# Slice stage of a graph network on one core: small attention's maximum and sums on ScalarE, z at the end of VectorE's step, output in the tokens' bank, slice tokens turned behind the logits

## The chip, the cores and the metric

The kernel runs on one core of one Trainium2 chip. The metric is the device time of the whole program in microseconds: 2829.99 us, the median of three runs from 2829.58 to 2830.06 us. An instruction stream runs on each engine: TensorE (PE, with its weight loads as PEld), VectorE (DVE), ScalarE (ACT), GpSimd (POOL) and SyncE (SP). They wait for each other by semaphores that the program sets by hand.

## What is computed

The input is x, 128 graphs of 128 nodes with 128 features in fp32, and an adjacency matrix for each graph. Four blocks are added to x in turn, each behind a layer norm: graph attention with an MLP, attention over slices, a graph convolution, and a mixture of experts. The change touches the second block alone, which is, for each graph with 8 heads of 64 columns:

```python
fx_mid = (x @ W_fx + b_fx).reshape(B, N, H, D).transpose(0, 2, 1, 3)
x_mid = (x @ W_x + b_x).reshape(B, N, H, D).transpose(0, 2, 1, 3)
slice_weights = jax.nn.softmax((x_mid @ W_slice + b_slice) / temp, axis=-1)
slice_token = jnp.einsum('bhnc,bhng->bhgc', fx_mid, slice_weights)
slice_token = slice_token / (slice_weights.sum(axis=2)[..., None] + 1e-05)
q, k, v = slice_token @ W_q, slice_token @ W_k, slice_token @ W_v
attn = jax.nn.softmax(jnp.einsum('bhgc,bhkc->bhgk', q, k) * SCALE, axis=-1)
out_slice = jnp.einsum('bhgk,bhkc->bhgc', attn, v)
out_x = jnp.einsum('bhgc,bhng->bhnc', out_slice, slice_weights)
return out_x.transpose(0, 2, 1, 3).reshape(B, N, INNER) @ W_out + b_out
```

The "small attention" is the softmax over 64 x 64 slices of each head (`attn`).

## The kernel before

All 128 graphs stay in on-chip memory as `X`. Five functions run one after the other: `attention_phase`, `mlp_phase`, `slice_phase`, `graph_phase`, `expert_phase`. At the end of `mlp_phase` some weights for the slice stage are made once, among them `wscore`, the product of W_q and W_k that turns slice tokens into keys (L588).

`slice_phase` is a software pipeline over graphs, written out by hand: in step t every engine works on several graphs, each at another point of its way, and does its pieces always in the order in which the code lists them. `run_steps` (L33) writes eight steps ahead, a loop of two steps, and seven behind. `live(known, n, ...)` says that a piece of step t works on graph t - n. There is no scheduler; a wait stands in front of the piece that needs it, and every piece behind it on that engine waits too. Some waits keep TensorE from writing a PSUM bank that another engine still reads.

TensorE's step t, by name and line:

1. logits of graph t-2 (L88 to L90, three matmuls of 512 columns) into `ps_l`
2. keys of graph t-4 (L882): the transposed tokens times `wscore`, into `ps_t`
3. transposes of `share`, the small attention's probabilities, of graph t-5 (L890) into `ps_h`
4. fx of graph t-2 (again L88 to L90) into `ps_f`
5. behind nine waits (L897 to L915), transposes of the slice weights `sw` of graph t-4 (L916)
6. scores of graph t-4 (L922), mixed of t-6 (L929), mt of t-5 (L936), u of t-3 (L947: the slice tokens before they are divided by their norm; `ps_u` lies in the bank of the logits)
7. transpose of z, the normalized graph t-1 (L956), into a bank of `ps_x`
8. output of graph t-6 (L965 and L968) into `ps_x`; it waits for ScalarE's copy of `mixed`
9. transposes of the tokens `tok` of graph t-3 (L976); it waits for VectorE's `tok`

ScalarE's step copies PSUM to SBUF and takes exponentials: key (L988), shareT (L993), expo (L998), mixed (L1005), att (L1010, the small attention's exponential over 256 columns at once), fx (L1016), zTh (L1021), mt (L1024), swT (L1029), tokT (L1034). VectorE's step: top and diff of the logits (L1051, L1055), z (L1062), statistics, top2 and diff2 of the scores (L1081, L1085), sum and reciprocal of expo (L1092, L1094), tok (L1098 to L1105), zTl (L1110), sum and reciprocal of att (L1116, L1118), the addition of the output to X (L1122), statistics. GpSimd's step: sw (L833), share (L840), rstd (L847, L850), and the statistics for the next stage (L856 to L860).

The maximum of the scores is taken off in VectorE (`diff2`), and ScalarE applies the factor 64 ** -0.5 in the exponential:

```python
nc.vector.reduce_max(top2[:, :, :], ps_s, AX.X).then_inc(s["top2_done"], 1)
...
nc.scalar.activation(att[:, :, :], diff2[:, :, :], ACT.Exp,
                     scale=float(C) ** -0.5).then_inc(s["att_done"], 1)
```

Of the kernel before, what the change touches and what calls it, by code (L numbers as in the profile page):

```python
# [15 lines left out]
D = 128  # L16
# [6 lines left out]
C = 64  # L23
# [487 lines left out]
def mlp_phase(nc, sem, sh, n_graphs):  # L511

    groups = n_graphs // GB
    with ExitStack() as ctx:
# [68 lines left out]
        def _(act):  # L583
# [4 lines left out]
            nc.scalar.activation(sh.wscore[:, :], ps_m, ACT.Copy).then_inc(wscore_copied, 1)  # L588
# [166 lines left out]
def slice_phase(nc, sem, sh, n_graphs):  # L755

    with ExitStack() as ctx:
# [6 lines left out]
        def ps(name, shape):  # L764
# [25 lines left out]
        diff2 = sb("s_diff2", [128, HP, C])  # L790
# [9 lines left out]
        ps_out, ps_z = ps_x[:, 0, 2 * C:2 * C + D], ps_x[:, 1, 2 * C:2 * C + D]  # L800
# [9 lines left out]
                 "scores_done top2_done diff2_done att_done sum2_done rsum2_done share_done share_turned shareT_done "  # L810
# [9 lines left out]
        def _(pool):  # L820
# [7 lines left out]
            def step(t, r, p, known):  # L828
                if live(known, 2, n_graphs):
# [13 lines left out]
                if live(known, 0, n_graphs):  # L843
                    pool.wait_ge(s["meanvar_done"], t + 1)
                    if since(known, 2):
                        pool.wait_ge(s["z_done"], t - 1)
                    nc.gpsimd.tensor_tensor(rstd[p][:, 1:2], meanvar[p][:, 1:2], sh.eps[:, 0:1],  # L847
                                            ALU.add).then_inc(s["eps_added"], 1)
                    pool.wait_ge(s["eps_added"], t + 1)
                    nc.gpsimd.tensor_tensor(rstd[p][:, 0:1], rstd[p][:, 1:2], sh.half_power[:, 0:1],  # L850
                                            ALU.pow).then_inc(s["rstd_done"], 1)
# [13 lines left out]
        def _(pe):  # L865
# [3 lines left out]
            def step(t, r, p, known):  # L869
                q = 1 - p  # L870
                if live(known, 2, n_graphs):

# [7 lines left out]
                if live(known, 4, n_graphs):  # L880
                    pe.wait_ge(s["tokT_done"], t - 3)
                    nc.tensor.matmul(ps_t[:, 0:2, :], sh.wscore[:, :], tokT[p][:, :, :], start=True,  # L882
                                     stop=True).then_inc(s["keys_done"], 1)
                if live(known, 5, n_graphs):
                    pe.wait_ge(s["share_done"], t - 4)
                    if since(known, 6):
                        pe.wait_ge(s["shareT_done"], t - 5)
                    pe.wait_ge(s["zT_done"], t - 1 if known is None else min(known - 1, n_graphs))
# [8 lines left out]
                if live(known, 4, n_graphs):  # L897
                    pe.wait_ge(s["key_copied"], t - 3)
                    if since(known, 5):
                        pe.wait_ge(s["diff2_done"], t - 4)  # L900
                    if since(known, 7):
                        pe.wait_ge(s["x_done"], t - 6)
                    if live(known, 2, n_graphs):
                        pe.wait_ge(s["zT_done"], t - 1)
                if live(known, 5, n_graphs):
                    pe.wait_ge(s["shareT_done"], t - 4)
                    if since(known, 7):
                        pe.wait_ge(s["mixed_copied"], t - 6)
                if live(known, 6, n_graphs):
                    pe.wait_ge(s["mt_copied"], t - 5)  # L910
                if live(known, 4, n_graphs):
# [5 lines left out]
                    last.then_inc(s["sw_turned"], 1)  # L917
                if live(known, 4, n_graphs):
# [31 lines left out]
                if live(known, 1, n_graphs):  # L950
                    pe.wait_ge(s["z_done"], t)
                    if since(known, 2):
                        pe.wait_ge(s["zT_done"], t - 1)
                    if live(known, 4, n_graphs):
                        pe.wait_ge(s["diff2_done"], t - 3)
                    nc.tensor.transpose(ps_z, z[:, :], sh.ident[:, :]).then_inc(s["z_turned"], 1)  # L956
                if live(known, 6, n_graphs):
                    pe.wait_ge(s["mixed_copied"], t - 5)
                    pe.wait_ge(s["swT_done"], t - 5)
                    if live(known, 4, n_graphs):  # L960
                        pe.wait_ge(s["diff2_done"], t - 3)
# [9 lines left out]
                if live(known, 3, n_graphs):  # L971
                    pe.wait_ge(s["tok_done"], t - 2)
                    if live(known, 4, n_graphs):
                        pe.wait_ge(s["key_copied"], t - 3)
                    for j in range(2):
                        last = nc.tensor.transpose(ps_t[:, j, :], tok[q][:, 2 * j:2 * j + 2, :], sh.ident[:, :])  # L976
                    last.then_inc(s["tok_turned"], 1)
# [3 lines left out]
        def _(act):  # L981
            def step(t, r, p, known):
                q = 1 - p
                if live(known, 4, n_graphs):
                    act.wait_ge(s["keys_done"], t - 3)
                    if since(known, 5):
                        act.wait_ge(s["scores_done"], t - 4)
                    nc.scalar.activation(key[:, :, :], ps_t[:, 0:2, :], ACT.Copy).then_inc(s["key_copied"], 1)  # L988
                if live(known, 5, n_graphs):
# [3 lines left out]
                    nc.scalar.activation(shareT[:, :, :], ps_h[:, :, :], ACT.Copy).then_inc(s["shareT_done"], 1)  # L993
                if live(known, 2, n_graphs):
# [3 lines left out]
                    nc.scalar.activation(expo[p][:, :, :], diff[p][:, :, :], ACT.Exp).then_inc(s["expo_done"], 1)  # L998
                if live(known, 6, n_graphs):
# [6 lines left out]
                if live(known, 4, n_graphs):  # L1006
                    act.wait_ge(s["diff2_done"], t - 3)
                    if since(known, 5):
                        act.wait_ge(s["share_done"], t - 4)
                    nc.scalar.activation(att[:, :, :], diff2[:, :, :], ACT.Exp,  # L1010
                                         scale=float(C) ** -0.5).then_inc(s["att_done"], 1)
# [5 lines left out]
                if live(known, 1, n_graphs):  # L1017
                    act.wait_ge(s["z_turned"], t)
                    if since(known, 3):
                        act.wait_ge(s["fx_done"], t - 2)  # L1020
                    nc.scalar.activation(zTh[q][:, :], ps_z, ACT.Copy).then_inc(s["zTh_done"], 1)  # L1021
# [8 lines left out]
                if live(known, 3, n_graphs):  # L1030
                    act.wait_ge(s["tok_turned"], t - 2)
                    if since(known, 5):
                        act.wait_ge(s["scores_done"], t - 4)
                    nc.scalar.activation(tokT[q][:, :, :], ps_t[:, 0:2, :], ACT.Copy).then_inc(s["tokT_done"], 1)  # L1034
# [3 lines left out]
        def _(dve):  # L1038
# [8 lines left out]
            def step(t, r, p, known):  # L1047
# [10 lines left out]
                if live(known, 1, n_graphs):  # L1058
                    dve.wait_ge(s["rstd_done"], t)
# [1260 lines left out]
```

## Time and profile before

| | |
|---|---|
| median of three runs | 2829.99 us (2829.58 to 2830.06) |
| span of the profiled execution | 2829.7 us |
| mean granted TensorE clock | 0.985 |
| TensorE busy | 2695.7 us, 95% of the span |
| VectorE busy | 1966.7 us, 70% |
| ScalarE busy | 1461.8 us, 52% |
| GpSimd busy | 1503.5 us, 53% |
| slice stage, VectorE's first maximum of scores to its last | 800.5 to 1630.1 us |

The times of the profiled execution are those of one run under the profiler; the runs without it agree with its span to 0.4 us. Rows of the timeline give the start, the duration, the engine, the line, what is written and what is read, and how many like instructions are merged in the row. A duration is longer than the time that an instruction holds its engine, because the next one may start while it ends; so what an instruction costs in a chain of like ones is read from start to start.

### The profile page before, as it was taken

Reading aid. Unit: us, or ns where it says so; the run is one execution under the profiler, and the core shown is the slowest. Engines: PE = TensorE matmul, PEld = TensorE weight load, DVE = VectorE, ACT = ScalarE, POOL = GpSimd, SP = SyncE. Lnnn points to the kernel's source line nnn. Section 1 sums busy time; section 2 is a strip of 40 time slices with the busy share of each in tenths; the row PEclk is TensorE's granted clock in tenths of the full one; section 3 lists DMA queues with packets and bytes.
Section 4 is the critical chain, followed back from the end, with each engine's and each line's share of the span. In section 5 each row is a group of like instructions: output and inputs, shape, how many; then the busy total and the mean of one; then the engine's idle time right before and its main releaser. Section 6 shows DMA issues by size and latency. Waiting matters only on the chain. (4 is left out here: it accounts for less than half of the span.)

```text
span 2829.7 us, 87893 instructions
## 1 busy us (share of the span) xinstructions
PE 2695.7 (95%) x28783; PEld 2136.2 (75%) x28784; DVE 1966.7 (70%) x6881; ACT 1461.8 (52%) x2930; POOL 1503.5 (53%) x2542
## 2 busy tenths in 40 slices
PE   8999999899989999999999989999998999999999
PEld 4666666599957777777777767777778999999988
DVE  5666666577778888888888858788874454545453
ACT  3444444455546666666666535455554444444444
POOL 5555555333234444444444427777761666666674
PEclk8999999999989999999999999999999999999999
DMA  1111111000000000000000011111232222222264
GB/s 52 30 37 30 36 31 46 3 0 0 0 1 0 0 0 0 0 0 0 0 0 0 1 35 58 57 56 56 85 115 61 75 76 81 75 80 77 71 195 147
DMA packets 158090, 118.01 MB, mean 42 GB/s; under 512 B 20150, under 2 KB 145593, under 8 KB 158010
## 3 DMA queue, kind: packets, MB, share of 16 engines
q1 hardware_dynamic: 140602, 81.02, 10.4%
q0 software_dynamic: 17408, 35.95, 3.8%
q8 instruction: 46, 0.75, 0.1%
q14 instruction: 34, 0.28, 0.0%
HBM read 68.36 MB, written 48.56 MB: 41 GB/s over the span
## 5 line engine op out<-in xcount | busy, mean ns | idle before, releaser
L2025 POOL DMA_INDIRECT token_y<-e_y,e_rows x288 | 294.7, 1023 | 78.8 <-issue 73.1
L2068 ACT ACTIVATE e_hidden<-e_ps,e_b1g 128x512 f32<-128x512 f32 x288 | 194.6, 688 | 258.4 <-PE e_ps L90 257.8
L833 POOL TENSOR_TENSOR s_sw<-s_expo,s_rsum 128x512 f32<-128x512 f32 x128 | 133.5, 1043 | 355.4 <-DVE s_rsum L1094 355.4
L1301 POOL DMA_INDIRECT sorted_z<-r_z,r_rows x256 | 264.8, 1034 | 66.6 <-issue 61.8
L2120 PE MATMUL e_ps<-expert_w,e_hidden 128*128 x2304 | 280.3, 275 | 0.0
L460 DVE TENSOR_REDUCE a_V<-a_ps_s 128x8 f32<-128x1024 f32 x128 | 156.9, 1226 | 176.8 <-PE a_ps_s L399 176.8
L2120 PEld LDWEIGHTS e_ps<-expert_w,e_hidden 128*128 128x128 f32 x2304 | 273.9, 192 | 6.3
L324 ACT ACTIVATE a_probT<-a_ps_st 128x1024 f32<-128x1024 f32 x128 | 131.2, 1025 | 203.3 <-PE a_ps_st L407 203.3
L399 PEld LDWEIGHTS a_ps_s<-a_nT 16*128 16x128 f32 x2048 | 136.2, 188 | 91.5 <-issue 55.6
L2197 DVE TENSOR_TENSOR e_biased<-e_ps,expert_b 128x512 f32<-128x512 f32 x72 | 49.8, 691 | 213.8 <-PE e_ps L2120 213.8
L399 PE MATMUL a_ps_s<-a_nT 16*128 16x128 f32 x2048 | 185.6, 299 | 11.1
L407 PE MATMUL a_ps_st<-a_topT,a_nT 17*128 17x128 f32 x2048 | 183.6, 297 | 0.1
L1005 ACT ACTIVATE s_mixed<-s_ps_v 128x512 f32<-128x512 f32 x128 | 76.5, 598 | 148.6 <-PE s_ps_v L936 145.8
L968 PE MATMUL s_ps_x<-s_mixed,s_swT 128*128 128x128 f32 x1024 | 143.6, 284 | 0.0
L407 PEld LDWEIGHTS a_ps_st<-a_topT,a_nT 17*128 17x128 f32 x2048 | 134.7, 186 | 1.1 <-issue 0.6
L608 ACT ACTIVATE m_hidden<-m_ps,m_b 128x512 f32<-128x512 f32 x128 | 86.8, 689 | 87.3 <-PE m_ps L90 87.2
L88 PE MATMUL e_ps<-e_zTh,e_w1h 128*128 128x512 f32 x288 | 126.5, 439 | 1.6 <-DVE e_zTl L2189 1.4
L968 PEld LDWEIGHTS s_ps_x<-s_mixed,s_swT 128*128 128x128 f32 x1024 | 127.1, 195 | 0.0
L660 PE MATMUL m_ps<-m_w,m_hidden 128*128 128x128 f32 x1024 | 124.4, 275 | 0.0
L660 PEld LDWEIGHTS m_ps<-m_w,m_hidden 128*128 128x128 f32 x1024 | 121.7, 192 | 2.8
L1361 PE MATMUL g_ps_h<-ident_bf 128*128 128x512 bf16 x476 | 120.6, 385 | 3.1 <-PEq L104 3.1
L263 POOL TENSOR_TENSOR X<-X,a_attn 128x128 f32 (+1 forms) x128 | 60.1, 470 | 112.7 <-DVE a_attn L455 110.4
(400 smaller groups left out, 8033.8 us busy)
## 6 DMA issues: line engine op xcount, KB each, us to landing
e_z<-sorted_z SPq DMA_DIRECT2D x72, 260.0 KB
c_y<-token_y SPq DMA_DIRECT2D x22, 512.0 KB, 4.1
X<-in_x_dram SPq DMA_DIRECT2D x32, 256.0 KB, 2.8
a_adj<-in_adj_dram SPq DMA_DIRECT2D x32, 256.0 KB, 2.8
g_adj<-in_adj_dram SPq DMA_DIRECT2D x32, 256.0 KB
out_dram<-X SPq DMA_DIRECT2D x32, 256.0 KB, 2.6
c_y_s<-token_y SPq DMA_DIRECT2D x10, 512.0 KB, 5.0
token_y<-e_y,e_rows POOLq DMA_INDIRECT x288
```

Of the source, the lines that this page charges most:

```text
L88: nc.tensor.matmul(out, weights[0], moving[0], start=start, stop=False)
L324: nc.scalar.activation(probT[b % 2][:, :, :, :], ps_st[:, :, :, :], ACT.Exp, scale=float(HD) ** -0.5).then_inc(s["prob_done"], 1)
L399: last = nc.tensor.matmul(ps_s[:, j, 2 * half + c, :], side, side, start=False, stop=(half == 1 and c == 1))
L407: last = nc.tensor.matmul(ps_st[:, j, 2 * (1 - half) + c, :], nT[own][rows, i, c, :], topT[(b + 2) % 4][rows, c, :], start=False, stop=(ha ...
L460: nc.vector.reduce_max(V[p][:, b, :, TOP].rearrange("p (c i j) -> p j i c", c=2, j=2), ps_s[:, :, :, :].rearrange("p j (i c) n -> p j i c ...
L660: last = nc.tensor.matmul(ps_2[1 - p][:, b, :], hidden[1 - p][:, f, b * T:(b + 1) * T], w2[:, f, :], start=(f == 0), stop=(f == FC - 1))
L833: nc.gpsimd.tensor_tensor(sw[p][:, :, :], expo[p][:, :, :], rsum[p][:, 1, :].unsqueeze(2).to_broadcast([T, HEADS, C]), ALU.mult).then_inc( ...
L968: last = nc.tensor.matmul(ps_out, swT[p][:, 2 * j + i, :], mixed[:, i, j, :], start=False, stop=(j == 1 and i == 1))
L1301: nc.gpsimd.indirect_dma_start(sh.sorted_z, bass.IndirectOffsetOnAxis(ap=rows[own][:, e * GB + piece:e * GB + piece + 1], axis=0), zr[own] ...
L2025: nc.gpsimd.indirect_dma_start(sh.token_y, bass.IndirectOffsetOnAxis(ap=rows[p][:, b:b + 1], axis=0), y[p][:, b, :], None).then_inc(y_scat ...
L2068: nc.scalar.activation(hidden[p][:, c, :], ps_1[c % 2][:, :], ACT.Gelu, bias=b1g[p][:, c:c + 1]).then_inc(s["hidden_done"], 1)
L2120: last = nc.tensor.matmul(ps_2[q][:, b, :], hidden[q][:, f, b * T:(b + 1) * T], w2[:, bass.ds(e, 1), f * D:(f + 1) * D].squeeze(1), start= ...
```

## The change

The pieces and their counts stay, but for the small attention. Its factor goes into `wscore`. VectorE takes the maximum with its sign turned, and ScalarE takes four exponentials of 64 columns straight from the scores in PSUM, each with its own maximum as a bias and its own sum written out; `diff2` and VectorE's sum are gone. TensorE turns the tokens one step later, behind the logits, and makes the keys behind fx; z is transposed in front of the scores into the tokens' bank `ps_t`, where the output now stands too. z is made at the end of VectorE's step for the step after, and GpSimd makes rstd first.

```diff
@@ mlp_phase
-            nc.scalar.activation(sh.wscore[:, :], ps_m, ACT.Copy).then_inc(wscore_copied, 1)
+            nc.scalar.activation(sh.wscore[:, :], ps_m, ACT.Copy, scale=float(C) ** -0.5).then_inc(wscore_copied, 1)
@@ slice_phase
-        ps_out, ps_z = ps_x[:, 0, 2 * C:2 * C + D], ps_x[:, 1, 2 * C:2 * C + D]
+        ps_z, ps_out = ps_t[:, 2, :], ps_t[:, 3, :]
@@ TensorE: tokens behind the logits
+                    pe.wait_ge(s["tok_done"], t - 3)
+                    pe.wait_ge(s["zT_done"], upto(-1))
...
+                        pe.wait_ge(s["key_copied"], t - 4)
...
+                        pe.wait_ge(s["x_done"], t - 6)
+                    for j in range(2):
+                        last = nc.tensor.transpose(ps_t[:, j, :], tok[p][:, 2 * j:2 * j + 2, :], sh.ident[:, :])
+                    last.then_inc(s["tok_turned"], 1)
@@ TensorE: keys behind fx, then the transposes of sw, then these waits and z
+                    pe.wait_ge(s["tokT_done"], t - 3)
+                    nc.tensor.matmul(ps_t[:, 0:2, :], sh.wscore[:, :], tokT[p][:, :, :], start=True,
+                                     stop=True).then_inc(s["keys_done"], 1)
...
+                if live(known, 4, n_graphs):
+                    pe.wait_ge(s["key_copied"], t - 3)
+                    if since(known, 5):
+                        pe.wait_ge(s["att_done"], t - 4)
...
+                    nc.tensor.transpose(ps_z, z[:, :], sh.ident[:, :]).then_inc(s["z_turned"], 1)
@@ ScalarE: behind zTh, in front of mixed
+                    act.wait_ge(s["top2_done"], t - 3)
...
+                    for i in range(2):
+                        for e in range(2):
+                            last = nc.scalar.activation(att[:, 2 * i + e, :], ps_s[:, i, e, :], ACT.Exp,
+                                                        bias=top2[:, i, e:e + 1],
+                                                        accum_out=rsum2[:, 0, 2 * i + e:2 * i + e + 1])
+                    last.then_inc(s["att_done"], 1)
@@ VectorE
-                    nc.vector.reduce_max(top2[:, :, :], ps_s, AX.X).then_inc(s["top2_done"], 1)
...
-                    nc.vector.tensor_tensor(diff2[:, :, :].rearrange("p (i e) k -> p i e k", e=2), ps_s,
-                                            top2[:, :, :].unsqueeze(3).to_broadcast([128, 2, 2, C]),
-                                            ALU.subtract).then_inc(s["diff2_done"], 1)
+                    nc.vector.reduce_max(top2[:, :, :], ps_s, AX.X, negate=True).then_inc(s["top2_done"], 1)
+                if live(known, 1, n_graphs):
+                    dve.wait_ge(s["zTh_done"], t)
+                    nc.vector.tensor_tensor(zTl[q][:, :], ps_z, zTh[q][:, :], ALU.subtract)\
+                      .then_inc(s["zT_done"], 1)
...
-                    nc.vector.reduce_sum(rsum2[:, 0, :], att[:, :, :], AX.X).then_inc(s["sum2_done"], 1)
...
+                if live(known, 0, n_graphs):
+                    dve.wait_ge(s["rstd_done"], t + 1)
```

On TensorE, one step inside the loop stood as follows before, from the keys to the next step's logits (its second half; `s_ps_x`, `s_ps_t` and so on are the PSUM tiles that are written):

```order
L88 MATMUL s_ps_l<-s_wlogit_high,s_zTh 128x512
L89 MATMUL s_ps_l<-s_wlogit_low,s_zTh 128x512
L90 MATMUL s_ps_l<-s_wlogit_high,s_zTl 128x512
L882 MATMUL s_ps_t<-s_tokT,wscore 128x256
L890 MATMUL s_ps_x<-ident,s_share 128x128 x2
...
L916 MATMUL s_ps_w<-ident,s_sw 128x128 x4
L922 MATMUL s_ps_x<-s_key,s_tokT 64x64 x8
...
L956 MATMUL s_ps_x<-ident,s_z 128x128
L965 MATMUL s_ps_x<-out_bias,ones_bf 128x128
L968 MATMUL s_ps_x<-s_mixed,s_swT 128x128 x4
L976 MATMUL s_ps_t<-ident,s_tok 128x128 x2
```

And the same step now:

```order
L88 MATMUL s_ps_l<-s_wlogit_high,s_zTh 128x512
L89 MATMUL s_ps_l<-s_wlogit_low,s_zTh 128x512
L90 MATMUL s_ps_l<-s_wlogit_high,s_zTl 128x512
L887 MATMUL s_ps_t<-ident,s_tok 128x128 x2
L895 MATMUL s_ps_x<-ident,s_share 128x128 x2
...
L904 MATMUL s_ps_t<-s_tokT,wscore 128x256
L911 MATMUL s_ps_w<-ident,s_sw 128x128 x4
L924 REGISTER_ALU
L927 MATMUL s_ps_t<-ident,s_z 128x128
L932 MATMUL s_ps_x<-s_key,s_tokT 64x64 x8
...
L969 MATMUL s_ps_t<-out_bias,ones_bf 128x128
L972 MATMUL s_ps_t<-s_mixed,s_swT 128x128 x4
```

The tokens' transposes left the end of the step for its front, the keys went behind fx, and z went from behind u to a place between the transposes of sw and the scores.

On ScalarE, the same step before, from the exponential of the logits on:

```order
L998 ACTIVATE s_expo<-s_diff 128x512
L1005 ACTIVATE s_mixed<-s_ps_v 128x512
L1010 ACTIVATE s_att<-s_diff 128x256
L1016 ACTIVATE s_fx<-s_ps_f 128x8x64
L1018 REGISTER_ALU
L1021 ACTIVATE s_zTh<-s_ps_x 128x128
L1024 ACTIVATE s_mt<-s_ps_v 128x256
L1029 ACTIVATE s_swT<-s_ps_w 128x512
L1034 ACTIVATE s_tokT<-s_ps_t 128x256
```

And now (in the program the subtracted maximum and the sums, `top2` and `rsum2`, are shown as `s_top` and `s_rsum`):

```order
L1000 ACTIVATE s_expo<-s_diff 128x512
L1002 REGISTER_ALU
L1005 ACTIVATE s_zTh<-s_ps_t 128x128
L1013 ACTIVATE s_att,s_rsum<-s_ps_x,s_top 128x64 x4
L1023 ACTIVATE s_mixed<-s_ps_v 128x512
L1028 ACTIVATE s_fx<-s_ps_f 128x8x64
L1031 ACTIVATE s_mt<-s_ps_v 128x256
L1036 ACTIVATE s_swT<-s_ps_w 128x512
```

zTh and att now stand in front of mixed, att is four instructions instead of one, and tokT went to the front of the step.

## Rows read from the trace of the kernel before

**Rows 1.** Windows view, the slice stage's full steps: busy us and counts by engine
```profile
core 0: us, PE busy (x) PEld busy (x) DVE busy (x) ACT busy (x) POOL busy (x), PEclk, DMA share, GB/s
832.00:1558.00 726.00, 699.70 (x9994) 533.75 (x9994) 633.27 (x2223) 443.69 (x1111) 356.59 (x778) 1.00 0.00 0
```

**Rows 2.** Waits view, 900 to 1500 us: us in total, times, longest us
```profile
PEld s_ps_w L916 <- issue: 47.1, 90, 0.6
...
PEld s_ps_l L88 <- issue: 20.6, 46, 0.4
PEld s_ps_t L976 <- DVE s_tok L1105: 16.5, 92, 0.2
```

**Rows 3.** Timeline, TensorE, 1000 to 1014 us: start, duration, line, out<-in
```profile
1000.25 0.40 PE L90 MATMUL s_ps_l<-s_wlogit_high,s_zTl 128*128 128x512 f32 x1
...
1007.30 0.59 PE L882 MATMUL s_ps_t<-s_tokT,wscore 128*128 128x256 f32 x2
1007.73 0.38 PE L890 MATMUL s_ps_x<-ident,s_share 128*128 128x128 f32 x2
1007.87 0.48 PE L88 MATMUL s_ps_f<-s_wfx_high,s_zTh 128*128 128x512 f32 x1
...
1008.42 0.40 PE L90 MATMUL s_ps_f<-s_wfx_high,s_zTl 128*128 128x512 f32 x1
1008.88 0.63 PE L916 MATMUL s_ps_w<-ident,s_sw 128*128 128x128 f32 x4
1009.43 0.46 PE L922 MATMUL s_ps_x<-s_key,s_tokT 64*64 64x64 f32 x16
...
1011.11 0.33 PE L956 MATMUL s_ps_x<-ident,s_z 128*128 128x128 f32 x1
1011.36 0.23 PE L965 MATMUL s_ps_x<-out_bias,ones_bf 128*128 128x128 bf16 x1
...
1012.55 0.44 PE L976 MATMUL s_ps_t<-ident,s_tok 128*128 128x128 f32 x2
1012.75 0.50 PE L88 MATMUL s_ps_l<-s_wlogit_high,s_zTh 128*128 128x512 f32 x1
...
1013.31 0.40 PE L90 MATMUL s_ps_l<-s_wlogit_high,s_zTl 128*128 128x512 f32 x1
1013.56 0.70 PE L882 MATMUL s_ps_t<-s_tokT,wscore 128*128 128x256 f32 x2
```

**Rows 4.** Timeline, ScalarE, the same stretch
```profile
1008.01 0.39 ACT L988 ACTIVATE s_key<-s_ps_t 128x256 f32<-128x256 f32 x1 [1.15 <-PE s_ps_t L882]
1008.29 0.38 ACT L993 ACTIVATE s_shareT<-s_ps_x 128x256 f32<-128x256 f32 x1
1009.04 0.63 ACT L998 ACTIVATE s_expo<-s_diff 128x512 f32<-128x512 f32 x1 [0.37 <-DVE s_diff L1055]
1010.71 0.60 ACT L1005 ACTIVATE s_mixed<-s_ps_v 128x512 f32<-128x512 f32 x1 [1.04 <-PE s_ps_v L936]
1011.20 0.41 ACT L1010 ACTIVATE s_att<-s_diff 128x256 f32<-128x256 f32 x1
...
1011.99 0.28 ACT L1021 ACTIVATE s_zTh<-s_ps_x 128x128 fp32r<-128x128 f32 x1
1012.14 0.40 ACT L1024 ACTIVATE s_mt<-s_ps_v 128x256 f32<-128x256 f32 x1
```

**Rows 5.** Timeline, VectorE, the same stretch
```profile
1008.31 0.69 DVE L1055 TENSOR_TENSOR s_diff<-s_ps_l,s_top 128x512 f32<-128x512 f32 x1
...
1009.96 0.42 DVE L1081 TENSOR_REDUCE s_top<-s_ps_x 128x4 f32<-128x256 f32 x1
1010.51 0.42 DVE L1085 TENSOR_TENSOR s_diff<-s_ps_x,s_top 128x256 f32<-128x256 f32 x1
```

**Rows 6.** Groups of instructions: busy us, mean ns of one, idle before
```profile
L608 ACT ACTIVATE m_hidden<-m_ps,m_b 128x512 f32<-128x512 f32 x128 | 86.8, 689 | 87.3 <-PE m_ps L90 87.2
```

**Rows 7.** Timeline, ScalarE in the graph convolution, 1762 us
```profile
1762.07 0.19 ACT L1581 ACTIVATE r_odds<-r_gap 128x4 f32<-128x4 f32 x1
1762.17 0.58 ACT L1589 ACTIVATE g_y<-g_ps_y 128x512 f32<-128x512 f32 x1
```

More of the change, by code:

```diff
@@ L828, in step @@
             def step(t, r, p, known):
+                if live(known, 0, n_graphs):
+                    pool.wait_ge(s["meanvar_done"], t + 1)
+                    if since(known, 2):
+                        pool.wait_ge(s["z_done"], t - 1)
+                    nc.gpsimd.tensor_tensor(rstd[p][:, 1:2], meanvar[p][:, 1:2], sh.eps[:, 0:1],
+                                            ALU.add).then_inc(s["eps_added"], 1)
+                    pool.wait_ge(s["eps_added"], t + 1)
+                    nc.gpsimd.tensor_tensor(rstd[p][:, 0:1], rstd[p][:, 1:2], sh.half_power[:, 0:1],
+                                            ALU.pow).then_inc(s["rstd_done"], 1)
                 if live(known, 2, n_graphs):
@@ L870, in step @@
                 q = 1 - p
+                upto = lambda n: t + n if known is None else min(known + n, n_graphs)
                 if live(known, 2, n_graphs):
@@ L970, in step @@
                     last.then_inc(s["out_done"], 1)
[L971 to L977, printed above, removed]
             run_steps(pe, step, n_graphs, LAG, PEEL)
@@ L984, in step @@
                 if live(known, 4, n_graphs):
[L985 to L988, printed above, removed]
+                    act.wait_ge(s["tok_turned"], t - 3)
+                    if since(known, 6):
+                        act.wait_ge(s["scores_done"], t - 5)
+                    nc.scalar.activation(tokT[p][:, :, :], ps_t[:, 0:2, :], ACT.Copy).then_inc(s["tokT_done"], 1)
                 if live(known, 5, n_graphs):
@@ L993, in step @@
                     nc.scalar.activation(shareT[:, :, :], ps_h[:, :, :], ACT.Copy).then_inc(s["shareT_done"], 1)
+                if live(known, 4, n_graphs):
+                    act.wait_ge(s["keys_done"], t - 3)
+                    if since(known, 5):
+                        act.wait_ge(s["scores_done"], t - 4)
+                    nc.scalar.activation(key[:, :, :], ps_t[:, 0:2, :], ACT.Copy).then_inc(s["key_copied"], 1)
                 if live(known, 2, n_graphs):
@@ L998, in step @@
                     nc.scalar.activation(expo[p][:, :, :], diff[p][:, :, :], ACT.Exp).then_inc(s["expo_done"], 1)
+                if live(known, 1, n_graphs):
+                    act.wait_ge(s["z_turned"], t)
+                    if since(known, 3):
+                        act.wait_ge(s["fx_done"], t - 2)
+                    nc.scalar.activation(zTh[q][:, :], ps_z, ACT.Copy).then_inc(s["zTh_done"], 1)
+                if live(known, 4, n_graphs):
+                    act.wait_ge(s["top2_done"], t - 3)
+                    if since(known, 5):
+                        act.wait_ge(s["share_done"], t - 4)
+                        act.wait_ge(s["rsum2_done"], t - 4)
+                    for i in range(2):
[4 more added lines that the diff above has]
+                    last.then_inc(s["att_done"], 1)
                 if live(known, 6, n_graphs):
@@ L1005, in step @@
                     nc.scalar.activation(mixed[:, :, :, :], ps_m, ACT.Copy).then_inc(s["mixed_copied"], 1)
[L1006 to L1011, printed above, removed]
                 if live(known, 2, n_graphs):
@@ L1057, in step @@
                                             ALU.subtract).then_inc(s["diff_done"], 1)
-                if live(known, 1, n_graphs):
-                    dve.wait_ge(s["rstd_done"], t)
-                    if since(known, 2):
-                        dve.wait_ge(s["z_turned"], t - 1)
-                    nc.vector.tensor_scalar(z[:, 1:D], X[:, bass.ds(t - 1, 1), 1:D].squeeze(1), meanvar[q][:, 0:1],
-                                            rstd[q][:, 0:1], ALU.subtract, ALU.mult).then_inc(s["z_done"], 1)
                 counted = live(known, 0, n_graphs) or live(known, 7, n_graphs)
@@ L1126, in step @@
                       .then_inc(s["after_stats_done"], 1)
+                if live(known, 0, n_graphs):
+                    dve.wait_ge(s["rstd_done"], t + 1)
+                    if since(known, 1):
+                        dve.wait_ge(s["z_turned"], t)
+                    nc.vector.tensor_scalar(z[:, 1:D], X[:, bass.ds(t, 1), 1:D].squeeze(1), meanvar[p][:, 0:1],
+                                            rstd[p][:, 0:1], ALU.subtract, ALU.mult).then_inc(s["z_done"], 1)
             run_steps(dve, step, n_graphs, LAG, PEEL)
```

68 lines of the change are left out of this document (16 added, 52 removed).

## Prediction

> **What bounds the kernel now.** I read the page's first part, then the slice stage alone in the windows view, then its waits, then one step of it engine by engine in the timeline. The page's engine rows name TensorE as the busiest engine of the whole program; the question is whether that holds where the change is made. In the slice stage it is busy 699.7 of 726 us at full clock, VectorE 633.3, ScalarE 443.7 [rows 1]: TensorE is the bound there, and what the change takes off VectorE is worth nothing unless TensorE waits for it. The same row of TensorE's timeline stands at 1000.25 and at 1013.31 [rows 3]: two steps take 13.06 us, one 6.53. TensorE's idle time is 726 - 699.7 = 26.3 us in 111 steps, 0.24 us a step, though short starts after each wait hide a little more of it in "busy". The waits view says where: the weight load of L916 (0.51 us a step, partly beside matmuls), the loop's end at L88 in every second step, and L976 for the tokens, 16.5/92 = 0.18 us [rows 2]. So a change that only takes TensorE's waits away could win at most about 0.24 x 126 = 30 us.
>
> The second thing to see is who feeds the last block of TensorE's step. ScalarE ends `mixed` at 1010.71 + 0.60 = 1011.31 [rows 4], and the output matmuls (L965) start at 1011.36 [rows 3]. They start 0.05 us behind that copy: already now it is just in time, with the transpose of z as the only work in front of it.
>
> **The change, part by part.**
>
> *Maximum and sums.* VectorE loses the subtraction (0.42 us) [rows 5] and a sum over as many elements, some 0.8 us a step together, on an engine that is not the bound: worth nothing by itself. ScalarE gets four exponentials of 64 columns in place of one of 256, each with a bias column and a sum written out. The trace shows none with both, so I build the price from start to start. A copy of 256 columns holds the engine 0.28 us (1008.01 to 1008.29), one of 128 0.15 (1011.99 to 1012.14) [rows 4], so one of 64 about 0.09. A bias column adds 0.09: 689 ns against the 0.60 of `mixed`, the same size [rows 4, 6]. The Exp took 0.41 against the 0.38 of a copy of that size [rows 4]: 0.025. A sum that is written out I price as one more tiny instruction on the engine: one of four columns holds it 0.10 us (1762.07 to 1762.17) [rows 7]. Together 0.305, four of them 1.22 us where one instruction of 0.41 stood [rows 4]. The ends are 0.09 each (bias and sum free) and 0.5 each (a 64-column instruction of 0.28 - 0.065 + 0.09 and one of 0.19 with no overlap at all). I take 0.305, since every row of ScalarE that stands back to back does overlap.
>
> The Trainium skill, "ScalarE: Activation LUTs", section What ACT_TABLE_LOAD costs, gives 186 ns plus 0.833 ns a column, 93 ns more for a pointer operand, and 93 ns of overlap back to back. The trace agrees on the pointer (0.09 us). As an estimate from that page each of the four is 239 ns before any price for its sum, and the cycle below would be 7.10 us, 2902 us in all. The skill's "VectorE: DVE Perf Modes", section Two Vector instructions with no wait between them, says that on VectorE an operation that writes out its accumulator is two instructions; no run here shows whether ScalarE does the same.
>
> *ScalarE's order.* The four now stand in front of `mixed`, not behind it. Before, `mixed` needed only TensorE's L936; now it stands behind top2, which needs the scores, VectorE's maximum and the four exponentials. Queued behind it on ScalarE are fx, mt and swT, which nobody needs before the next step; TensorE's output waits for `mixed` itself. This is the term that decides.
>
> *TensorE's order.* The tokens' transposes move behind logits, keys behind fx, and between keys and the wait for their copy lie only the four transposes of sw (0.55 us, 1008.88 to 1009.43) [rows 3], where two transposes and fx stood before (0.14 + 0.80 = 0.94 us, worked out below). The wait for `shareT` is then long satisfied, and so is the one for tok. The loop's end comes behind eight output matmuls that are already queued, so its 0.45 us (20.6/46) [rows 2] in every second step goes too. But what is late next is the key copy, and then `mixed`.
>
> *z early, output in the tokens' bank, GpSimd's rstd first, the scale in the score weight.* z is made at the end of the step before, and TensorE asks for it only behind the transposes of sw; rstd needs only the statistics of the same step; the x addition, over half as many elements as the maximum of 0.42 us [rows 5], fits into the 0.81 us of logits that stand before the tokens' transposes into the same bank. I cost these at nothing. Were the addition late, the price would be at most those 0.42 us a step.
>
> *The sum.* In the changed order one cycle runs through TensorE, ScalarE, VectorE and back, and nothing else in the step is as long:
> - output to next logits: 1011.36 to 1012.55 less the 0.18 of waiting for tok: 1.01 [rows 2, 3]
> - logits 1012.75 to 1013.56: 0.81; two pairs of transposes at 0.14 (1007.73 to 1007.87): 0.28; fx 0.55 + 0.25 (1007.87 to 1008.42, last matmul as 1013.31 to 1013.56): 0.80 [rows 3]
> - start of keys to start of the copy, 1007.30 to 1008.01: 0.71; copy 0.39 [rows 3, 4]
> - from the copy's end (1008.40) to TensorE's next matmul took 0.48 with one register step and eight more waits to pass (1008.88) [rows 3, 4]; now fewer are left behind it, half: 0.25 (ends 0.1 and 0.48)
> - z, as 1011.11 to 1011.36: 0.25; scores' start to VectorE's maximum, 1009.43 to 1009.96: 0.53; maximum 0.42; to ScalarE 0.04 (1008.31 + 0.69 to 1009.04) [rows 3 to 5]
> - four exponentials: 1.22; `mixed` 0.60; to TensorE 0.05 [rows 4]
>
> That is 6.14 + 1.22 = 7.36 us against 6.53: 0.83 us more in each step that has both scores and output. Scores belong to steps 4 to 131 and output to steps 6 to 133, so 126 steps: 0.83 x 126 = 104 us. The other stages stay. Seen from TensorE: from the scores' start it can reach the output after about 1.7 us (1009.43 to 1011.11), `mixed` comes after 0.53 + 0.42 + 0.04 + 1.22 + 0.60 + 0.05 = 2.86; about 1.1 us of idling there and some 0.3 before z, less the waits that go.
>
> The profiled execution's span is 2829.7 us and the runs' median 2829.99, so what lies around the span is about 0.3 us. 2830 + 104 = **2934 us**.
>
> **The rivals.**
> - *The sums are dear.* Each sum holds ScalarE for a tiny instruction's whole 0.19 us [rows 7]: 0.395 each, 6.14 + 1.58 = 7.72 us, +150: 2980. For it: in rows 7 the neighbour reads something else, and no row shows an instruction that takes up what the one just before it has summed. Against it: that neighbour did start after 0.10.
> - *The sums are free.* Written by the same instruction: 0.205 each, 6.96 us, +54: 2884. For it: no row shows a sum that costs.
> - *The chain is hidden: no change.* At 0.09 each the cycle is 6.50 us, 4 us less in all: 2826. It needs bias and sum to cost nothing, against the rows of both [rows 6, 7].
> - *Faster, the other side.* TensorE's waits go and nothing takes their place: 0.24 us a step, 30 us: 2800. The place is L969's wait for `mixed`; it decides at 4 exponentials below 6.53 - 6.14 = 0.39 us in all. For it: 0.51 us of L916's idle weight load, 0.45 of the loop's end and 0.18 of L976 are real and do go [rows 2], and parts of my cycle may run closer together than their rows. Against it: even four bare copies of 64 columns take 0.36 us.
>
> **How the numbers follow.** Forecast 0.56; dear sums 0.19; free sums 0.15; hidden 0.04; faster 0.06. About 0.2% is what a measurement of this kernel can tell from no change. Faster 0.06, within it 0.04, slower 0.90. The range holds the forecast, the free and the dear sums with a little on each side: 2878 to 2988. With the ends of the wait after the key copy (-0.15 to +0.23 us a step, -19 to +29 us) the forecast alone is 2915 to 2963.
>
> **What would show it.** In the changed trace: TensorE's load of out_bias (L969) waits for ScalarE's `mixed` about 1 us in every step; a start-to-start of some 0.3 us for each of the four att instructions; ACT's mixed no longer waits for TensorE; a wait of TensorE at z (L927) for the key copy; the loop's end at L88 and the token wait gone; VectorE about 100 us less busy, with long waits for the scores; the steps 7.2 to 7.5 us apart. Wrong would be a step below 6.6 us, an output that does not wait for `mixed`, or a loss that stands in another stage.

## The result, and the profile after

The changed kernel took 2948.8 us in the median of four runs: 1.041 times the kernel before, 95% interval 1.039 to 1.043. The forecast was 2934 us, in a range of 2878 to 2988. In the profiled executions the span went from 2829.7 to 2947.0 us, 117.3 more.

Two rows of VectorE say where they lie. The small attention's maximum (`s_top<-s_ps_x`) and the graph convolution's reciprocal (`g_rdeg`) run in every step of their stages, and their first and last starts give each stage's length. Count, shortest, median and longest in ns, first and last start in us; the kernel before, then the changed one:

```profile
L1081 DVE TENSOR_REDUCE s_top<-s_ps_x x128: 390/424/425, 800.5 to 1630.1; 128x4 f32<-128x256 f32 x128
L1674 DVE RECIPROCAL g_rdeg<-g_rdeg x32: 162/165/178, 1653.8 to 2080.3; 128x4 f32<-128x4 f32 x32
```

```profile
L1079 DVE TENSOR_REDUCE s_top<-s_ps_x x128: 423/425/426, 802.8 to 1720.3; 128x4 f32<-128x256 f32 x128
L1670 DVE RECIPROCAL g_rdeg<-g_rdeg x32: 163/165/179, 1743.8 to 2197.5; 128x4 f32<-128x4 f32 x32
```

Over 127 intervals a step of the slice stage went from 829.6/127 = 6.53 us to 917.5/127 = 7.22. The graph convolution begins 90.0 us later. But its last row is 117.2 us late: 27.2 us were lost in a stage whose code the change does not touch, 453.7 us between its rows in place of 426.5.

*The slice stage.* The windows view of the changed kernel answers to [rows 1], the waits to [rows 2]:

```profile
832.00:1558.00 726.00, 590.51 (x9001) 483.58 (x9002) 488.47 (x1805) 499.16 (x1706) 320.66 (x701) 1.00 0.00 0
```

```profile
PEld s_ps_t L969 <- ACT s_mixed L1023: 104.6, 83, 1.3
PE s_ps_t L969 <- ACT s_mixed L1023: 93.3, 83, 1.2
ACT s_att L1013 <- DVE s_top L1079: 50.7, 83, 0.6
PEld s_ps_t L927 <- issue: 35.7, 83, 0.4
PE s_ps_t L927 <- ACT s_key L995: 18.4, 83, 0.2
```

TensorE is no longer the bound: 590.5 us busy of 726. In each of the 83 steps looked at, the output (L969) waits about 1.1 us for `mixed`, and z (L927) 0.2 us for the key copy. The loop's end at L88 and the wait for VectorE's `tok` are gone from the list. ScalarE's timeline of one step shows why `mixed` is late, in answer to [rows 4]:

```profile
1012.38 0.31 ACT L1013 ACTIVATE s_att<-s_ps_x,s_top 128x64 f32<-128x64 f32 x1 [0.60 <-DVE s_top L1079]
1012.59 0.19 ACT L1013 ACTIVATION_READ_ACCUMULATOR s_att<-s_ps_x,s_top 128x1 f32 x1
1012.68 0.30 ACT L1013 ACTIVATE s_att<-s_ps_x,s_top 128x64 f32<-128x64 f32 x1
...
1013.26 0.32 ACT L1013 ACTIVATE s_att<-s_ps_x,s_top 128x64 f32<-128x64 f32 x1
1013.46 0.21 ACT L1013 ACTIVATION_READ_ACCUMULATOR s_att<-s_ps_x,s_top 128x1 f32 x1
1013.55 0.61 ACT L1023 ACTIVATE s_mixed<-s_ps_v 128x512 f32<-128x512 f32 x1
```

Each exponential that hands out its sum is followed by an instruction of its own, the read of the accumulator. From exponential to exponential it is 0.29 to 0.30 us (1012.38 to 1012.68), four take 1.17 (1012.38 to 1013.55), and only then `mixed` starts.

*The graph convolution.* The stage's clock and busy times, before and after:

```profile
1653.00:2083.00 430.00, 411.04 (x3067) 324.38 (x3067) 342.14 (x1804) 217.13 (x397) 287.82 (x369) 0.98 0.23 70
```

```profile
1743.00:2200.00 457.00, 424.93 (x3066) 338.27 (x3067) 341.89 (x1803) 216.54 (x397) 287.25 (x369) 0.94 0.22 66
```

VectorE has the same work (342 us). One turn of the stage's loop on VectorE, which holds four steps, before and after, at the same place:

```profile
1817.02 0.27 DVE L1842 TENSOR_TENSOR r_either<-r_chosen 128x32 bf16<-128x32 f32 x1
1818.05 1.12 DVE L1661 SCALAR_TENSOR_TENSOR g_sum<-g_ps_g,g_rdeg,g_sum 128x128 f32<-128x128 f32 x4 [0.77 <-PE g_ps_g L1431]
```

```profile
1907.17 0.26 DVE L1838 TENSOR_TENSOR r_either<-r_chosen 128x32 bf16<-128x32 f32 x1
1910.50 0.35 DVE L1657 SCALAR_TENSOR_TENSOR g_sum<-g_ps_g,g_rdeg,g_sum 128x128 f32<-128x128 f32 x1 [3.07 <-issue]
1912.74 0.87 DVE L1657 SCALAR_TENSOR_TENSOR g_sum<-g_ps_g,g_rdeg,g_sum 128x128 f32<-128x128 f32 x3 [1.89 <-issue]
```

After it VectorE stands still for 3.07 us and, one instruction later, for 1.89, and waits for nothing that the profile knows ("issue"): 4.96 us in place of the 0.77 that it waited for TensorE. The queue rows on the page of the profile name a suspect: packets, MB, share; before, then after.

```profile
q14 instruction: 34, 0.28, 0.0%
```

```profile
q14 instruction: 54, 0.44, 0.1%
```

A queue that carries instructions, some 8 KB a packet, has 20 packets more. In the built programs an instruction takes 64 bytes, so a packet holds 128. There the body of this loop on VectorE stands at instructions 1291 to 1636 before and 1270 to 1615 after, since the slice stage ahead of it lost 21. Cut at multiples of 128, it lay in three pieces (from 1280) and now touches four. That was the theory with which the experiments began.

### The profile page after: what moved, and what is told of

It reads as the page before. It is cut to its first block and busy times, and to the rows that moved or that the text cites. A ratio compares the mean times of both kernels' runs of the same rounds, so it can differ in the third digit from the quotient of the medians.

```text
span 2947.0 us, 88355 instructions
## 1 busy us (share of the span) xinstructions
PE 2662.0 (90%) x28783; PEld 2155.1 (73%) x28784; DVE 1861.4 (63%) x6625; ACT 1586.3 (54%) x3826; POOL 1503.8 (51%) x2542
## 5 line engine op out<-in xcount | busy, mean ns | idle before, releaser
L1013 ACT ACTIVATE s_att<-s_ps_x,s_top 128x64 f32<-128x64 f32 x512 | 154.0, 313 | 78.9 <-DVE s_top L1079 78.9
L832 POOL TENSOR_TENSOR s_rstd<-s_meanvar,eps 128x1 f32<-128x1 f32 x128 | 24.5, 191 | 315.6 <-DVE s_meanvar L1072 315.6
L969 PE MATMUL s_ps_t<-out_bias,ones_bf 128*128 128x128 bf16 x128 | 29.4, 230 | 143.3 <-ACT s_mixed L1023 143.3
L1112 DVE TENSOR_TENSOR X<-X,s_ps_t 128x128 f32 (+1 forms) x128 | 37.0, 289 | 177.3 <-PE s_ps_t L972 177.3
L972 PE MATMUL s_ps_t<-s_mixed,s_swT 128*128 128x128 f32 x1024 | 142.8, 283 | 0.0
L969 PEld LDWEIGHTS s_ps_t<-out_bias,ones_bf 128*128 128x128 bf16 x128 | 12.3, 96 | 160.8 <-ACT s_mixed L1023 160.8
L88 PE MATMUL e_ps<-e_zTh,e_w1h 128*128 128x512 f32 x288 | 126.7, 440 | 1.4 <-DVE e_zTl L2185 1.4
L972 PEld LDWEIGHTS s_ps_t<-s_mixed,s_swT 128*128 128x128 f32 x1024 | 126.4, 194 | 0.0
```

Source lines behind the costliest of these rows:

```text
L88: nc.tensor.matmul(out, weights[0], moving[0], start=start, stop=False)
L972: last = nc.tensor.matmul(ps_out, swT[p][:, 2 * j + i, :], mixed[:, i, j, :], start=False, stop=(j == 1 and i == 1))
L1013: last = nc.scalar.activation(att[:, 2 * i + e, :], ps_s[:, i, e, :], ACT.Exp, bias=top2[:, i, e:e + 1], accum_out=rsum2[:, 0, 2 * i + e:2 ...
```

## The experiments

All times are medians; the kernel before took 2829 to 2832 us beside each. (In the texts quoted here, a loop that "begins at 1268" or "at 1278" is counted from two instructions ahead of its body.)

**e1, e2: VectorE's program moved, nothing else.** Both add copies of one column, run once ahead of the slice stage's steps: 16 to the changed kernel, 32 to the kernel before.

```diff
+        extra = sb("s_extra", [T, 16])
...
+            for k in range(16):
+                nc.vector.tensor_copy(extra[:, k:k + 1], sh.eps[:, 0:1])
```

> The changed kernel with 16 more copies of one column on VectorE, once, ahead of the slice stage's steps. Theory (VectorE's program): the change made VectorE's program shorter ahead of the graph-convolution stage, by 21 instructions of the built program, and so moved the loop of that stage from instructions 1289 to 1636 to 1268 to 1615; counted in pieces of 128 instructions (64 bytes each, the 8 KB that a packet of the instruction queue q14 carries) the loop touched three pieces before and touches four now, and is fetched anew at every turn. With 16 more it lies at 1284 to 1631, in three pieces again: 2922 us (2917 to 2927), 27 less than the changed kernel, q14 back to about 34 packets, the turns of 19 us in the graph stage gone, the slice stage as in the changed kernel. Rival (the graph stage is longer because of what the slice stage leaves it: later data, another clock): 2949 to 2951 us, with 54 packets.

> The kernel before with 32 such copies on VectorE ahead of the slice stage, nothing else. Theory (VectorE's program): the graph stage's loop moves from 1289 to 1636 to 1321 to 1668, from three pieces of 128 instructions to four, and that stage loses the 27 us with nothing of the change in it: 2857 us (2850 to 2865, about 2 of them the copies), q14 near 54 packets. Rival (the loss needs the change): 2830 to 2833 us, 34 packets.

Sixteen copies that compute nothing used made the changed kernel 24 us faster: 2924.7 us (ratio to before 1.0325, interval 1.031 to 1.034). q14 carries 35 packets, and the stage takes 429.9 us between its rows:

```profile
L1673 DVE RECIPROCAL g_rdeg<-g_rdeg x32: 162/165/178, 1741.5 to 2171.4; 128x4 f32<-128x4 f32 x32
```

The 32 copies made the kernel before slower, without any of the change: 2846.0 us (1.0044, 1.0027 to 1.006; ten runs from 2834.9 to 2851.2, beside 2826.2 to 2837.5), 54 packets, and the waits without a releaser on the same instruction:

```profile
DVE g_sum L1664 <- issue: 12.4, 4, 3.2
```

Its size was missed (2857 expected): it has one stall of 3.1 to 3.2 us a turn, where the changed kernel mostly has two, and its graph convolution takes 439.2 us between the rows (1657.7 to 2096.9), 13 more than before, not 27. Why one stall and not two is open.

**e9, e10: where the edge is.** The same edit on the changed kernel with 9 and with 10 copies.

> The changed kernel with 9 copies on VectorE ahead of the slice stage: the body of the graph stage's loop on VectorE then runs from instruction 1279 to 1624 of the built program, its first instruction the last one of a piece of 128. Theory (the body has to lie in three pieces): it touches four, q14 carries 54 packets, and the time stays that of the changed kernel, 2945 to 2955 us. Rival (what counts is how much of the body lies outside three pieces, and one instruction is nothing): 2922 to 2930.

> The same with 10 copies, one more: the body begins at 1280, which is 10 times 128, and ends at 1625, in three pieces. Theory: 34 or 35 packets and 2922 to 2930 us, some 25 less for one instruction more. Rival (some other effect of the copies): the same time as with 9.

2920.7 and 2919.2 us, both with 35 packets. The exact edge that I had forecast is wrong: a body from 1279 already has no loss. Bodies from 1270 (the changed kernel) and 1271 (e7 below) are fetched anew, those from 1279 to 1291 are not, that from 1323 is. Three pieces of 128 from an edge between 1272 and 1279 fit all of them, so the pieces are counted from a few instructions off the start of my count. Where exactly was not tried. By that edge the body of e2 ends 6 to 13 instructions inside a fourth piece, and that of the changed kernel begins 2 to 9 ahead of the first of its three.

**e3: mixed ahead of the exponentials again**, ScalarE's order alone:

```diff
+                if live(known, 6, n_graphs):      # mixed, from behind the exponentials
+                    ...
                 if live(known, 4, n_graphs):
                     act.wait_ge(s["top2_done"], t - 3)
...
-                if live(known, 6, n_graphs):
-                    ...
```

> The changed kernel with one thing undone: in ScalarE's step the copy of mixed stands ahead of the four exponentials again. Theory of the prediction (a ring from the output over the logits, key copy, scores, VectorE's maximum, four exponentials and mixed back to the output): the maximum, the hop and the exponentials leave the ring, mixed begins when the mt matmuls end, some 1.2 us after the scores instead of 2.2, and a step takes 6.2 to 6.5 us in place of 7.25: 2814 to 2854 us, with the graph stage's 27 us still in it (VectorE's program is the same). Rival one (the four exponentials bound wherever they stand, as they also hold the fx and mt copies behind them, and the share's turn waits for att): a step of 6.9 to 7.25 us, 2905 to 2949. Rival two (the prediction's order of the small attention was harmless and the other moves of the change cost it): within 10 us of 2949.

2863.5 us (1.010, 1.007 to 1.013): 85 us of the loss gone by one block that moves on one engine. The slice stage is as long as before the change, 825.3/127 = 6.50 us a step, and the weight load's wait for `mixed` falls from 104.6/83 = 1.26 us to 25.6/92 = 0.28:

```profile
L1079 DVE TENSOR_REDUCE s_top<-s_ps_x x128: 424/425/425, 806.2 to 1631.5; 128x4 f32<-128x256 f32 x128
...
PEld s_ps_t L969 <- ACT s_mixed L1012: 25.6, 92, 0.3
...
L1670 DVE RECIPROCAL g_rdeg<-g_rdeg x32: 162/165/178, 1656.6 to 2121.0; 128x4 f32<-128x4 f32 x32
```

The step came out at the upper end of the 6.2 to 6.5 us expected, so the moves of the change save nothing that is left over. The graph stage's loss stays in this kernel, as VectorE's program is the same (54 packets); at 464.4 us between its rows it is even 10.7 larger here, and the time missed its range (2814 to 2854) by 9.5 us.

**e4: the sums on VectorE**, ScalarE's exponentials without `accum_out`, VectorE's `reduce_sum` back:

> The changed kernel without the sums on ScalarE: the four exponentials keep their bias but hand out no sum, and VectorE sums att again ahead of the reciprocal. Theory (the chain holds the exponentials; with the read behind each, a pair has a pitch of 0.29 us, 0.09 of it from the read's start to the next exponential): 4 times 0.09 to 0.11 leaves the chain, a step of 6.8 to 6.9 us, 2893 to 2913 us. Rival one (each read costs its whole 0.20 us): 0.8 us a step, 2848. Rival two (the exponentials are not in the ring): 2949. VectorE's graph loop begins at instruction 1278 here, 10 further than in the changed kernel and still in four pieces: by the theory of the program the 27 us and 54 packets stay.

2873.6 us (1.014, 1.012 to 1.016). Two things went: 0.38 us a step (868.6/127 = 6.84), as the theory had it, and 20 packets (its body begins at 1280, q14 is back at 34), against what I had written of it; so the time is below the expected range. Four exponentials now take 0.80 us up to `mixed`, not 1.17:

```profile
1011.18 0.93 ACT L1012 ACTIVATE s_att<-s_ps_x,s_top 128x64 f32<-128x64 f32 x4 [0.62 <-DVE s_top L1077]
1011.98 0.61 ACT L1021 ACTIVATE s_mixed<-s_ps_v 128x512 f32<-128x512 f32 x1
```

So a sum costs 0.09 us, and an exponential with bias 0.20.

**e5: both repairs**, mixed first and the 16 copies.

> The changed kernel with both repairs: mixed ahead of the four exponentials on ScalarE, and the 16 copies on VectorE ahead of the slice stage. Theory (two causes that add: the place of mixed in the slice stage, the place of VectorE's program in the graph stage): the slice stage as with mixed first alone, 6.55 us a step, q14 at about 34 packets, the graph stage as in the kernel before: 2829 to 2838 us. Rival (the graph stage is slow with mixed first for another reason, such as the clock of 0.97 in that run): about 2863.

2829.7 us, 0.9998 of before (0.9988 to 1.0008), 35 packets. The two causes add up, and by the interval nothing over 3 us is left of the loss.

**e6: mixed first, and the sums on VectorE.**

> Mixed ahead of the exponentials, and the sums back on VectorE (four exponentials with bias, no sum). VectorE's graph loop begins at 1278, where the run with the sums on VectorE had 34 packets, so the graph stage is expected as before. Theory (with mixed first the exponentials still end late enough that TensorE waits for share, 0.15 to 0.3 us a step): they end 0.37 us sooner, that wait goes, 6.3 to 6.5 us a step: 2805 to 2828 us. Rival (with mixed first the exponentials are off the path, and the sums are free either way): 2829 to 2838, as with mixed first and the copies.

2841.0 us (1.0034, 1.001 to 1.006), 834.8/127 = 6.57 us a step. My theory fell: TensorE's wait for share did not go, and the step is 0.08 us longer than in e5 (823.8/127 = 6.49). The exponentials do still hold something in e5: VectorE's reciprocal of the sums waits 28.7/92 = 0.31 us a step for them. With the sums on VectorE that wait is gone, but a sum of 0.42 us stands in its place, and what VectorE does next, the addition to X, is no earlier. TensorE's weight load for the tokens' transposes waits for that addition in every second step, and in the others with no releaser shown: together 22.1/92 = 0.24 us a step in e5 and 28.3/91 = 0.31 in e6. That is about the difference, though no run tests it by itself. The lines of e5, then of e6:

```profile
DVE s_rsum L1111 <- ACT s_att L1021: 28.7, 92, 0.3
PEld s_ps_t L888 <- issue: 11.7, 46, 0.3
PEld s_ps_t L888 <- DVE X L1115: 10.4, 46, 0.2
```

```profile
PEld s_ps_t L887 <- issue: 15.6, 45, 0.4
PEld s_ps_t L887 <- DVE X L1112: 12.7, 46, 0.3
```

**e7, e8: the two halves of the change alone.** e7 is the kernel before with the new small attention in the old order, e8 the changed order (mixed first) with the old small attention.

> The kernel before with the change's small attention alone (scale in the score weights, negated maximum, four exponentials with bias and sum on ScalarE, no subtraction and no sum on VectorE), in the order and the banks of before: mixed still ahead of the exponentials, and the turn of z and the output in the banks of the scores, so that TensorE waits there for the exponentials' end instead of VectorE's subtraction. Theory (in the old banks the exponentials gate z's turn, which moves from some 1.5 us behind the scores to 2.9): 7.8 to 8.1 us a step, 150 to 190 us, and the graph stage loses about 27 (VectorE's loop begins at 1269): 2990 to 3050 us. Rival (the old order hides them behind mixed): slice stage within 10 us, 2850 to 2865.

> The changed kernel's order, banks and moves, with the small attention of before (VectorE subtracts and sums, one exponential on ScalarE, behind mixed). Theory (the moves shorten the ring and only the four exponentials ahead of mixed lengthened it): the ring holds scores, mt matmuls, mixed, output: 6.3 to 6.6 us a step, graph stage as before (loop at 1288): 2800 to 2838 us. Rival (VectorE, with the subtraction between the maximum and the low half of z, becomes late for the output's wait on zT): 6.7 to 7.0 us a step, 2845 to 2885.

e7 took 3032.8 us (1.072, 1.070 to 1.074), 1000.2/127 = 7.88 us a step: in the old banks z's turn (L955) waits for the exponentials' end, as expected. e8 took 2897.2 us (1.024, 1.021 to 1.026), 886.7/127 = 6.98 a step, the rival's size. But it is not the output that waits, as the rival had it: TensorE's logits wait for the tokens, which VectorE makes behind its subtraction and reads from the logits' bank. From the output's start to the logits it is 1.34 and 1.47 us in two steps of e8, 1.02 and 0.93 in two of e5, most of the 0.49 by which their steps differ. One wait of each, e7 first:

```profile
PE s_ps_x L955 <- ACT s_att L1012: 108.7, 77, 1.5
```

```profile
PE s_ps_l L88 <- DVE s_tok L1101: 19.8, 85, 0.3
```

Each half loses time alone, and together, with `mixed` in its old place, they break even (e5). Neither of these two waits is on e5's list: the new banks take the exponentials out of z's way, and VectorE's lighter step brings the tokens in time.

**e11, e12: a version that beats both.** In e5 TensorE's weight load still waits for share ahead of fx, 0.3 us in every second step by the line below and 0.2 in the others:

```profile
PEld s_ps_x L896 <- issue: 13.5, 46, 0.3
```

e11 is e5 with share's turn on TensorE moved behind fx, and e12 is e11 with the sums on VectorE in place of the copies:

```diff
-                    for j in range(2):       # share's turn, with its waits, from ahead of fx
-                        last = nc.tensor.transpose(ps_h[:, j, :], ...)
                     split_matmul(nc, ps_f[:, :, :], ...).then_inc(s["fx_done"], 1)
+                    for j in range(2):       # to behind it, ahead of the keys
+                        last = nc.tensor.transpose(ps_h[:, j, :], ...)
```

> A candidate for a version that beats both: mixed first, 16 copies on VectorE, and on TensorE the turn of share moved from ahead of fx to behind it, ahead of the keys. Theory (with mixed first TensorE waits 0.15 to 0.3 us a step for share, and fx, which waits for nothing then, can stand in that gap; the copy of shareT still lies on ScalarE ahead of the key copy, beside the keys' matmul): 6.25 to 6.4 us a step in the slice stage, 2793 to 2812 us. Rival (the wait moves to the key copy, which stands behind the later shareT copy on ScalarE): 2825 to 2835, or up to 2850 where the key copy is late by the whole shareT copy.

> The same candidate with the sums on VectorE in place of the copies (loop body from 1280). Theory (with share's turn late, the end of the exponentials no longer matters, and VectorE's sum only loads VectorE, which cost 0.08 us a step with mixed first): 5 to 15 us above the candidate with the sums on ScalarE, 2800 to 2825. Rival (ScalarE's chain of exponentials, fx, mt, swT and tokT copies bounds the candidate): 5 to 25 us below it.

2798.4 us, 0.9896 of before (0.987 to 0.993), and 2807.9 for e12 (0.992, 0.989 to 0.995), both as the theory had it. A step of e11 is 797.3/127 = 6.28 us; its wait for share is gone, those for the key copy (L928) and `mixed` (L970) stay:

```profile
PEld s_ps_t L928 <- issue: 41.0, 95, 0.5
PEld s_ps_t L970 <- ACT s_mixed L1013: 26.8, 96, 0.3
```

## Why the prediction was right, and where it was not

*What decides.* "This is the term that decides", of the place of `mixed` behind the exponentials: shown. L969 waits 1.1 us for `mixed` in each step, as worked out, and e3 takes back the slice stage's whole loss by that place alone.

*The exponentials.* Forecast 0.305 each, measured 0.29. The parts were differently sized: 0.20 for an exponential with bias (0.205 in the sum) and 0.09 for the sum (0.10), from e4. The rivals on the sums are settled by the same rows: neither dear (the read's duration is 0.19 to 0.21, but it overlaps its neighbours) nor free. What the Trainium skill, "VectorE: DVE Perf Modes", section Two Vector instructions with no wait between them, says of VectorE, that a written accumulator is a second instruction, these rows show of ScalarE too.

*The size in the slice stage.* 104 us forecast, 90 measured, as the cycle was 7.23 us in one half of the loop and 7.26 in the other (1014.22 to 1021.48), not 7.36. Three terms were too long: output to logits 1.01 against 0.93 (1014.22 to 1015.15), keys to the copy 0.71 against 0.63 (1017.08 to 1017.71), and the four exponentials 1.22 against 1.17. Two were too short: the two pairs of transposes took 0.37 and not 0.28 (1015.93 to 1016.30), as the pair of tokens holds TensorE 0.23 and not 0.14, and the scores to the maximum took 0.53 in one half and 0.62 in the other (1018.57 to 1019.19).

```profile
1014.22 0.23 PE L969 MATMUL s_ps_t<-out_bias,ones_bf 128*128 128x128 bf16 x1 [1.08 <-ACT s_mixed L1023]
1015.15 0.47 PE L88 MATMUL s_ps_l<-s_wlogit_high,s_zTh 128*128 128x512 f32 x1
...
1015.93 0.40 PE L887 MATMUL s_ps_t<-ident,s_tok 128*128 128x128 f32 x2
...
1016.30 0.47 PE L88 MATMUL s_ps_f<-s_wfx_high,s_zTh 128*128 128x512 f32 x1
...
1017.08 0.59 PE L904 MATMUL s_ps_t<-s_tokT,wscore 128*128 128x256 f32 x2
1017.71 0.39 ACT L995 ACTIVATE s_key<-s_ps_t 128x256 f32<-128x256 f32 x1 [0.62 <-PE s_ps_t L904]
...
1018.57 0.46 PE L932 MATMUL s_ps_x<-s_key,s_tokT 64*64 64x64 f32 x16
1019.19 0.42 DVE L1079 TENSOR_REDUCE s_top<-s_ps_x 128x4 f32<-128x256 f32 x1 [0.54 <-PE s_ps_x L932]
...
1021.48 0.23 PE L969 MATMUL s_ps_t<-out_bias,ones_bf 128*128 128x128 bf16 x1 [1.17 <-ACT s_mixed L1023]
```

*What was costed at nothing.* z early, the output's bank, rstd first and the x addition. One wait of the changed kernel names the x addition: the weight load for the tokens' transposes, into the bank where the output stands too.

```profile
PEld s_ps_t L887 <- DVE X L1112: 9.5, 42, 0.2
```

It costs TensorE next to nothing: the transposes start 0.24 to 0.28 us behind the last matmul of the logits, where one such matmul takes 0.25 [rows 3]. No wait names the others, and e5 bounds all of them together, with the gains, at 0 to within 3 us.

*The step that failed.* "The other stages stay." The graph convolution lost 27 us, though its code did not change. The prediction had named "a loss that stands in another stage" as a sign of being wrong, and of these 27 us the sign is right. e1, e2 and e5 show the cause: the place of its loop in VectorE's program. The 14 us too many in the slice stage and the 27 missing here gave 2934 for 2949: the closeness is in part luck. Of the 27, the stalls at four turns of the loop make about 19 (a step there of 18.5 to 19.1 us between the reciprocals, not 14.2). Most of the rest, 6.5 us, stands in two steps of 17.0 us instead of 13.7 behind the first such turn, where the granted clock is low. Windows of the changed kernel (same columns as the windows above):

```profile
1870.00:1905.00 35.00, 33.23 (x246) 25.52 (x246) 28.82 (x153) 17.96 (x33) 25.98 (x34) 1.00 0.20 61
1905.00:1915.00 10.00, 6.25 (x56) 5.43 (x55) 4.61 (x27) 2.64 (x6) 5.80 (x8) 0.95 0.15 44
...
1930.00:1945.00 15.00, 14.23 (x78) 11.33 (x75) 9.13 (x53) 6.18 (x12) 10.28 (x13) 0.77 0.15 49
...
1990.00:2010.00 20.00, 19.13 (x151) 15.97 (x151) 15.56 (x90) 10.15 (x19) 15.35 (x20) 1.00 0.18 53
```

TensorE had only 6.25 us of work in the 10 us of the stall. Its granted clock was 1.00, the level of 2.4 GHz, from 1870 to 1905; from 1930 to 1945 it was 0.77, a mix with the level of 1.2 GHz, and from 1990 it was 1.00 again. That the stall caused it was not tested by itself: e1, without stalls, has 0.98 over the stage, as before, but it dips too, to 0.90 from 1870 to 1905.

The rivals "hidden" and "faster" are out: a slice step takes 7.22 us, not 6.5 or less.

## What to carry to other kernels

Ask of an instruction that goes ahead of another on an in-order engine what the one behind it feeds: here 1.17 us of exponentials in front of a copy that TensorE waits for cost 90 us, and behind it nothing (e3, e5). And compare the whole trace, not the stage that was edited: a stage behind it can be slower because its loop lies elsewhere in an engine's program. Here waits without a releaser at the loop's turn and more packets on the instruction queue were the signs; some instructions whose results nobody uses, run once ahead of it, were the test and the cure.

## What was not expected of the hardware

A loop body of 346 instructions on VectorE ran without being fetched anew from instruction 1279, 1280, 1286, 1290 and 1291, with 34 or 35 packets on q14, and with 54 packets and stalls of mostly 3 to 5.5 us a turn from 1270, 1271 and 1323. The stalls stand at four turns, so the 20 packets more are five a turn, one more than the four pieces that such a body touches. The Trainium skill, "Advanced Engine Details and Errata", section ISA Cache, gives an engine such as this 32 KB in two lines of 256 instructions. As an estimate from that page the body, 346 instructions of 64 bytes or 22 KB, would fit by its size wherever it lies; these runs show that its place decides. The lines do not explain the runs by themselves: 0.28 MB in 34 packets are 8 KB, 128 instructions, each; and by lines of 256 from the same edge a body from 1323 to 1668 would lie in two, like that of the kernel before, yet it was refetched (e2). Three pieces of 128 fit all the runs. Why three and not four, which would be the 32 KB, they don't show; five packets a turn would fit a piece that is fetched ahead of need, but no run tests that.
